# One mask product per PSUM bank, the residual added on TensorE, rows of ones by DMA, and the first scan inputs on VectorE

## The reference

```python
xn = _layernorm(x)
x = x + _L0_attn_ref(xn, ...) + _L0_ffn_ref(xn, ...)

# the first: a selective scan of 512 steps (512 channels x 16 states)
xz = xn @ W_in; x_in, z = split(xz)
x_in = silu(conv4(x_in) + b_conv)
dbc = x_in @ W_xproj; dt = softplus(dbc[:64] @ W_dt + b_dt)
state = clip(state * exp(clip(dt * A)) + x_t * dt * B_t, -10, 10)
y_t = sum_n(state * C_t) + D * x_t
out = (y * silu(z)) @ W_out

# the second: attention with 16 heads, then a mixture of experts
x = xn + mla(rmsnorm(xn))            # causal: scores masked above the diagonal
x = x + shared_expert(rmsnorm(x)) + sum over the top 2 of 7 experts
```

## Time and profile before

| | |
|---|---|
| median of 3 runs | 4429.94 us (4425.78 to 4437.9) |
| the profiled execution | 4428.19 us, of which the span of the trace is 4426.1 us |
| stage 1 | 0 to about 1705 us |
| stage 2 | to 2181 us |
| stage 3 | 2181 to 4426 us |
| busy over the span | PE 3749.4 us (85%), DVE 2973.9 (67%), ACT 2502.8 (57%), POOL 2202.3 (50%) |
| mean granted TensorE clock | 0.93 |

### The profile page before, as it was taken

The page is one execution under the profiler, slowest core; times in us unless marked ns, Lnnn a source line. Parts: engine busy times, 40 slices in busy tenths (PEclk is TensorE's granted clock), DMA queues, the critical chain, the costliest instruction groups (busy, mean ns, idle before and its releaser), DMA issues.

```text
span 4426.1 us, 71771 instructions
## 1 busy us (share of the span) xinstructions
PE 3749.4 (85%) x22840; PEld 2837.4 (64%) x22840; DVE 2973.9 (67%) x5485; ACT 2502.8 (57%) x6473; POOL 2202.3 (50%) x1120
## 2 busy tenths in 40 slices
PE   4888888888888875999879888889998898888886
PEld 2444444444444434777658888878887888788776
DVE  4454444554545422222269999999999999999997
ACT  1443344334444341333278777788787787777773
POOL 2223333333333321000067777777777777777774
PEclk8899899999999987999989999999999999999998
DMA  2322232222322214666522222222222222222221
GB/s 85 96 82 83 79 95 82 84 79 93 97 88 85 81 51 117 212 213 208 161 89 92 76 87 78 80 87 87 75 92 85 78 92 76 87 80 78 87 82 36
DMA packets 285739, 419.89 MB, mean 95 GB/s; under 512 B 77397, under 2 KB 249814, under 8 KB 262808
## 3 DMA queue, kind: packets, MB, share of 16 engines
q1 hardware_dynamic: 273048, 381.12, 26.5%
q0 software_dynamic: 12288, 33.57, 2.2%
HBM read 330.63 MB, written 83.17 MB: 93 GB/s over the span
## 4 chain that ended last, share of the span: by engine, by line
POOL 22%; issue 10%; DVE 9%; PE 8%; ACT 1%; DVEq 0%; POOLq 0%; DMA 0%; SPq 0%; ACTq 0%
POOL m_ub L1516 18%; PE m_Y L1870 7%; DVE m_PR L1720 2%; DVE m_S L1728 2%; DVE m_PR L1728 2%; DVE m_S L1720 2%; POOL m_th_z L1501 1%; POOL m_yg L1526 1%; DVE m_ub L1705 1%; POOL m_dtx L1495 1%; ACT m_dA L1626 0%; PE m_F L1881 0%; PE m_F L1832 0%; PE m_F L1806 0%; DVEq L1719 0%
## 5 line engine op out<-in xcount | busy, mean ns | idle before, releaser
L1516 POOL TENSOR_TENSOR m_ub<-m_Bb,m_dtx 128x2048 f32<-128x2048 f32 x256 | 1157.5, 4544 | 436.3 <-PE m_Y L1870 429.9
L1626 ACT ACTIVATE m_dA<-m_dt,m_a_neg 128x128 f32<-128x128 f32 x4096 | 1211.1, 388 | 168.1 <-DVE m_S L1728 166.9
L1870 PE MATMUL m_Y<-m_ub,m_ident 128*128 128x128 f32 x8192 | 1040.9, 293 | 204.4 <-DVE m_ub L1705 204.4
L1870 PEld LDWEIGHTS m_Y<-m_ub,m_ident 128*128 128x128 f32 x8192 | 1022.7, 208 | 218.2 <-DVE m_ub L1705 218.2
L539 ACT ACTIVATE f_pt<-f_X 128x512 f32<-128x512 f32 (+1 forms) x704 | 372.2, 554 | 725.2 <-PE f_X L831 674.8
L615 DVE TENSOR_REDUCE f_nm<-f_Y 128x1 f32<-128x512 f32 (+3 forms) x896 | 434.1, 531 | 365.7 <-PE f_Y L825 339.6
L1720 DVE SCALAR_TENSOR_TENSOR m_PR<-m_dA,m_S 128x512 f32<-128x512 f32 x512 | 355.8, 695 | 123.1 <-POOL m_ub L1516 52.2
L824 PE MATMUL f_Y<-f_kst,f_qst 96*128 96x512 bf16 (+3 forms) x1024 | 281.9, 331 | 107.1 <-DVE f_nm L615 89.9
L1720 DVE SCALAR_TENSOR_TENSOR m_S<-m_dA,m_PR 128x512 f32<-128x512 f32 x512 | 355.1, 694 | 12.1
L1728 DVE CUSTOM_DVE_ANT_1 m_PR<-m_PR,m_ub 128x512 f32<-128x512 f32 x512 | 353.8, 691 | 0.2 <-DVE m_PR L1720 0.2
L1728 DVE CUSTOM_DVE_ANT_1 m_S<-m_S,m_ub 128x512 f32<-128x512 f32 x512 | 353.8, 691 | 0.0
(11 more groups left out here) (229 smaller groups left out, 6530.7 us busy)
## 6 DMA issues: line engine op xcount, KB each, us to landing
m_Bb<-m_bc_dram SPq DMA_DIRECT2D x64, 1024.0 KB, 4.5
m_Cb<-m_bc_dram SPq DMA_DIRECT2D x64, 1024.0 KB, 4.6
f_parts_dram<-f_parts SPq DMA_DIRECT2D x32, 768.0 KB, 4.1
f_kst<-f_parts_dram SPq DMA_DIRECT2D x192, 128.0 KB, 2.6
f_qst<-f_parts_dram SPq DMA_DIRECT2D x192, 128.0 KB, 2.6
e_rows<-sorted_rows SPq DMA_DIRECT2D x70, 256.0 KB, 2.7
e_wg<-Wg SPq DMA_DIRECT2D x70, 256.0 KB, 2.9
e_wu<-Wu SPq DMA_DIRECT2D x70, 256.0 KB, 3.9
```

Source lines behind the costliest of these rows:

```text
L1516: pool.tensor_tensor(ub[:, h, i, :, :], Bb[:, s, :, :], dtx[:, par, m, None, s * SN:(s + 1) * SN].to_broadcast([P, NST, SN]), ALU.mult).th ...
L1626: last = act.activation(dA[:, h, i, n, :], dtt[:, par, m, s * SN:(s + 1) * SN], ACT.Exp, scale=a_neg[:, m, n:n + 1])
L1870: last = pe.matmul(Y[:, i * SN:(i + 1) * SN], ident[:, :], ub[:, h, i, n, :], start=False, stop=(n == NST - 1), skip_group_check=True)
```

## The change

Four edits:

- **Masks.** The score products of a bank come first and one product `identb` x mask (`hide`) covers all diagonal blocks of the bank: its moving operand is the mask, repeated without a copy, and its output the blocks at their distance. In a pair of heads 8 mask products become 5, in a group of four 16 become 11: 84 for a sequence in place of 128, 704 fewer in all. The first product of a bank alone has `start=True`.
- **Residual.** `project_out` gets a product `ident` x `res` at the end of each row block. ScalarE copies the bank to `ot` (`copy_out`) after the decays of unit 2; the addition on VectorE is gone.
- **Ones.** The two memsets of VectorE are gone. ScalarE issues six DMAs at its start, each of which fills one row of `kst` (16 KB) from `onesb`, 128 pieces of 128 bytes. The waits of TensorE and ScalarE for `w_loaded` move to the first use of a weight.
- **First unit.** VectorE makes `dt`, `dtx` and the inputs of unit 0 of chunk 0; POOL goes on with unit 1.

```diff
-            pe.matmul(bank[:, c0:c0 + n], qst..., kst..., start=True, stop=False)
-            return pe.matmul(bank[:, c0 + qb * P:c0 + n], identb[:, :], mask_q[:, :], start=False, stop=True)
+            pe.matmul(bank[:, c0:c0 + n], qst..., kst..., start=(c0 == 0), stop=False, skip_group_check=True)
...
+        def hide(bank, c0, step, count, mask):
+            blocks = bank[:, c0:c0 + (count - 1) * step + P]
+            if count > 1 and step > P:
+                blocks = bank[:, :].rearrange("p (a s) -> p a s", s=step)[:, 0:count, c0:c0 + P]
+            elif count > 1:
+                blocks = blocks.rearrange("p (a s) -> p a s", s=step)
+            src = mask[:, None, :].to_broadcast([P, count, P]) if count > 1 else mask[:, :]
+            return pe.matmul(blocks, identb[:, :], src, start=False, stop=True, skip_group_check=True)
...
-        act.wait_ge(w_loaded, W_ALL)
+        act.wait_ge(const_ready, N_CONST_FIRST)
+        for p in range(2):
+            for q in range(PARTS):
+                act.dma_start(kst[p][KS + q:KS + q + 1, :, :]..., onesb[:, 0:NH * SEQ // P]).then_inc(q_scaled, 16)
...
-        for p in range(2):
-            dve.memset(kst[p][KS:KS + PARTS, :, :], 1.0).then_inc(q_scaled, 1)
...
+        def copy_out(c):
+            act.wait_ge(outp_done, c + 1)
+            act.wait_ge(ot_stored, 16 * c)
+            act.activation(ot[:, :, :], F[2][:, :, :], ACT.Copy).then_inc(ot_done, 1)
...
                 decays(c, par, 2)
+                copy_out(c - 1)
...
-                slots[1][1] = lambda: add_res(c - 1)
...
+            pe.wait_ge(res_loaded, 16 * (c + 1))
             pe.wait_ge(ot_done, c)
             for j in range(TT):
...
                 for k in range(TOPK):
-                    last = pe.matmul(F[2][:, j, :], wdiag[:, k, j, :], yg[:, k, j, :], start=False, stop=(k == TOPK - 1))
+                    pe.matmul(F[2][:, j, :], wdiag[:, k, j, :], yg[:, k, j, :], start=False, stop=False)
+                last = pe.matmul(F[2][:, j, :], ident[:, :], res[:, j, :], start=False, stop=True)
...
         log_rest(0)
+        dve.wait_ge(sp_ln, 1)
+        dve.tensor_tensor(sp_u..., sp_u..., sp_r..., ALU.add).then_inc(sp_sub, 1)
+        dve.tensor_tensor(dtt[:, 0, :, :], sp_u..., sp_v..., ALU.subtract).then_inc(dt_ready, 1)
+        dve.tensor_tensor(dtx[:, 0, :, :], x2[:, 0, :, :], dtt[:, 0, :, :], ALU.mult).then_inc(dtx_ready, 1)
+        for i in range(2):
+            dve.tensor_tensor(ub[:, 0, i, :, :], Bb..., dtx..., ALU.mult).then_inc(u_ready[0], 1)
```

60 lines of the change are left out of this document (36 added, 24 removed).

## The result

On the first chip the kernel before takes 4429.94 us and the changed kernel 4457.64 us (medians of five runs; 4444.66 to 4483.84 for the changed one). The ratio is 1.0073, with a 95% interval from 1.0046 to 1.0100: slower, as forecast, but by 27.7 us between the medians, and 32 us by the ratio, where 16 were forecast (4446, a ratio of 1.0036, which lies under the interval). In later comparisons on another chip it is 1.0054 [1.0031, 1.0077], about 24 us.

What follows compares the result with a forecast made beforehand. It took a path over VectorE, TensorE and POOL to bound each chunk's first half in stage 3. 4428.2 - 5.5 - 2 - 2.3 + 25.8 - 0.6 + 0.8 = 4444.4, as a median 4446 us (+0.37%); range 4418 to 4462.

Steps and rivals of the forecast that it cites:

- the start of stage 3: First unit's inputs on VectorE: the scan starts 2.3 us earlier, with the decays last; -2.3 us, ends -3 and 0.
- the late copy: Rival: ScalarE's copy comes late and holds back TensorE at `F[2]`; 0.5 us a chunk, 4461 us; chance 5%.
- the clock: TensorE's clock, 2.4 GHz or 1.2 GHz after idling; counted in the forecast's own range, 4434 to 4458 us.
- The path to unit 2: Stage 3, first half of a chunk: VectorE, TensorE, then POOL set 33.5 us from unit 0 to unit 2.
- The rival in which VectorE's steps set the end: Stage 3: without the addition each chunk loses 0.6 us, 18.6 in all; 4402 us; chance 8%.
- The rival of products at 1.2 GHz: The residual's new products run at 1.2 GHz, being later behind an idle time; 4472 us; chance 7%.
- The products' term: Residual's two products on TensorE, ahead of unit 0's sums: 0.86 us a chunk in chunks 1 to 30, +25.8 us.
- the rival in which part is absorbed: Part of the products' 0.86 us is absorbed; if half the loss is given back, 4433 us; chance 17%.
- The start of stage 1: Without VectorE's memsets the first reciprocal comes earlier, between 6.3 and 3.7 us; -5.5 us.
- Stage 1 as a whole: Two terms: -5.5 us at its start without memsets, -2 us for the merged masks; 7.5 us less.
- +0.2: End of stage 3: -0.6 us for the addition taken away in chunk 31, +0.8 us in the tail.

Runs made afterwards that it cites:

- `add_kept`: The kernel before with the two products ident x res added in project_out and VectorE's addition kept, so the residual is added twice; 1.0042 of the kernel before.
- `res_first_dt_late`: The changed kernel with the residual's products first in project_out, dt_proj after unit 0's sums, 12 instructions fewer ahead of VectorE's loop; 0.9928 of the kernel before, 4400.2 us.
- `after_fewer`: The changed kernel with 12 instructions fewer on VectorE ahead of its loop in stage 3; 1.0041 of the kernel before.
- `masks_alone`: The kernel before with the merged mask products alone; 0.9994 of the kernel before.

## Why the prediction was wrong, and what of it held

**The step that failed: the start of stage 3, and what it left out.** Under that head I costed the first unit's inputs on VectorE by their durations and by what waits for them, took -2.3 us, and asked nothing of the loop behind them. The effect on the loop so went into the sum as nothing. They lengthen the code ahead of VectorE's loop by five instructions, the two dropped memsets shorten it by two (and four waits come in), and the loop begins at a place where each of its 13 turns stands still for another 0.72 us: +9.4 us in gaps, and 14 to 17 us over chunks 1 to 30 against the three kernels that only move the loop elsewhere. I had thought of edits only in terms of time on an engine; this one has its price in a loop that it doesn't touch. The range reached to 4462 for other reasons (the late copy, the clock) and held the 4457.6 us by luck.

**The 2.3 us themselves don't last either.** From the memset of the states to the scan's first step the kernel before takes 54.92 us (2181.06 to 2235.98), the changed one 52.27 (2164.79 to 2217.06) and 51.23 in its second profile, and the decays are last: 2.7 to 3.7 us less. So far the forecast holds. But chunk 0 then takes longer: 75.6 to 82.3 us in the twelve kernels that have the first unit on VectorE, 80.0 on average, and 75.2 to 80.8 in the six that don't, 76.7 on average; in most of them VectorE waits ahead of a gate for TensorE's sums. Chunk 1 starts 131.5 us after the start of the stage on average in both groups. The rows that answer to the earlier trace rows:

```profile
2203.72 1.23 DVE L1787 TENSOR_TENSOR m_sp_u<-m_sp_u,m_sp_r 128x1024 f32<-128x1024 f32 x1 [1.53 <-ACT m_sp_u L1628]
2204.97 1.22 DVE L1790 TENSOR_TENSOR m_dt<-m_sp_u,m_sp_v 128x1024 f32<-128x1024 f32 x1
2206.23 1.23 DVE L1793 TENSOR_TENSOR m_dtx<-m_x,m_dt 128x1024 f32<-128x1024 f32 x1
2207.49 8.81 DVE L1797 TENSOR_TENSOR m_ub<-m_Bb,m_dtx 128x2048 f32<-128x2048 f32 x2
2217.06 0.70 DVE L1744 SCALAR_TENSOR_TENSOR m_PR<-m_dA,m_S 128x512 f32<-128x512 f32 x1 [0.75 <-ACT m_dA L1641]
```

VectorE's estimate of 1.2 us for 1024 columns holds. Its two inputs take 8.8 us where I had said some 4.6, but not evenly: the first takes 2.29 us, as forecast, the second 6.61 us, and POOL's two beside them 6.62 and 6.57 us where they take 4.5 each in the kernel before. The ends come at 2209.79 (VectorE), 2214.16 (POOL), 2216.31 (VectorE) and 2220.69 (POOL), in steps of 4.4, 2.1 and 4.4 us, about what one such product takes POOL, VectorE and POOL by itself. The two engines do them in turn, in all twelve kernels that have this pair. It didn't matter here: VectorE's end at 2216.3, and the decays 0.76 us later.

**The path to unit 2 was right.** All that it was read from (the 0.90 us of idle, the gapless stretch on TensorE, POOL's start on half the sums) holds: idle time 2.42 us, 34.56 us from unit 0 to unit 2 in chunk 12, a copy that holds up nobody, an addition that is worth nothing where it stood. The rival in which VectorE's steps set the end was wrong for this kernel; it becomes true of the first half of a chunk as soon as `dt_proj` leaves the path. The rival of products at 1.2 GHz, and the one with the late copy, didn't come about.

**The products' term: more on the path, less in the end.** 0.86 us a chunk were 0.94 to 0.95 to unit 2 (`add_kept` against the kernel before), +28.2 us over 30 chunks instead of +25.8. I had let all of it reach the end of the chunk. The second halves gave 8.1 us back, and the whole comes to +20.1 us in the trace and +18.5 [+7, +30] in the comparison. So the rival in which part is absorbed came about in part. Where the 0.08 us on the path come from wasn't looked into.

**The start of stage 1 was right.** The reciprocal comes at 18.69 us, 4.64 earlier than in the earlier trace rows, between the ends of 3.7 and 6.3:

```profile
18.23 0.42 DVE L637 TENSOR_SCALAR f_w_q<-f_w_q 64x512 f32<-64x512 f32 x1 [11.70 <-DMA f_ln<-w_ln]
18.69 0.18 DVE L640 RECIPROCAL f_sc<-f_sc 128x4 f32<-128x4 f32 x1
```

VectorE waits for the loads alone, as said; these come 2 us later than the 16 us that I took from the earlier trace rows. The six DMAs of the ones run among them, with 864 packets on a queue of their own, not 768.

**Stage 1 as a whole is open within some 9 us.** Stage 3 begins at 2192 us on average in six kernels with the old stage 1 (2181 to 2201) and at 2179 in eleven with the new one (2165 to 2198): 13 us less, uncertain by 9, where 7.5 were forecast. Part of the spread goes with the granted clock: of two kernels with the same new stage 1, the last `f_xs` begins at 1688.7 us in `res_first_dt_late` with 0.92 granted from 50 to 1650 us, and at 1717.4 us in `after_fewer` with 0.90. Between the two profiles first compared it was 16.3 us, and I took the surplus for the masks; `masks_alone` didn't bear it out.

**The sum, with what was measured.** Stage 1 -13, up to chunk 1 nothing, chunks 1 to 30 +35 (36.9 and 33.4 in the two traces of the changed kernel; 20 of it for the products and 14 to 17 for the loop's place), the tail -1: +21 us, which is 1.0047. The comparisons gave 1.0054 and 1.0073, each with an interval that holds it. The forecast had -7.5, -2.3, +25.8 and +0.2, +16 in all. That its miss is no larger is partly luck: the 14 to 17 us that the sum didn't have were in part made up by what the products gave back and by a stage 1 that won more than forecast. And a difference of 12 us between two medians of five is by itself within the spread of executions; what carries the missing term is its 13 gaps, not the total.

## To carry to other kernels

Follow the idle time of the busiest engine back to the last event of its path, and price new work by the place where it is put: the same four records cost 0.94 us on the way to unit 2 behind the last gate and nothing while that gate was being written. Then follow the shift to the end of the period, since the second half of a chunk gave part of it back. Before reordering, read every wait of the instructions that share a buffer with the moved one, and look first for work on the path whose result isn't needed yet (moving `dt_proj` alone gave 19 us by the medians). When code ahead of a tight loop changes its length, look at the loop's first instructions in the trace, and at the packets of the instruction queues, even though the loop is unchanged.
